# Own step tables for the first two and the last three graph pairs, and an fp32 weight product at the head, in a two-layer attention kernel

## The reference

```python
h = max(layernorm(x), 0)
q, k, v = h @ Wq0 + bq0, h @ Wk0 + bk0, h @ Wv0 + bv0          # 8 heads of 64
w = softmax(q @ k.T / 8 + (adj == 0) * -1e9)                    # per head
x = x + w @ v
h = max(layernorm(x), 0)
rel = adj.T * ((h @ Wq1.T) @ (h @ Wk1.T).T)
rel = rel / norm(rel, axis=2)
x = x + rel @ (h @ Wv1.T)
```

## Time and profile before

| | |
|---|---|
| median of three runs | 2456.46 us |
| the profiled execution's own time | 2453.71 us |
| its span | 2451.9 us |
| busy: TensorE, VectorE, ScalarE, GpSimd | 98%, 59%, 69%, 53% |
| granted TensorE clock, mean | 0.994 |
| first matmul, last matmul's group starts | 19.24 us, 2445.97 us |
| share of line 656 (all split products) in the chain that ended last | 78% of the span into B, 7% into O |

### The profile page before, as it was taken

How to read it: one execution, slowest core, us unless ns; L and a number is a source line. 1 busy time by engine, 2 the same in 40 slices (tenths; PEclk the granted TensorE clock), 3 DMA queues, 4 the chain that set the end, 5 groups by cost and what they waited for, 6 DMA issues and landing times.

```text
span 2451.9 us, 53549 instructions
## 1 busy us (share of the span) xinstructions
PE 2395.6 (98%) x19252; PEld 1302.3 (53%) x19252; DVE 1442.2 (59%) x4435; ACT 1686.0 (69%) x4111; POOL 1300.1 (53%) x1159
## 2 busy tenths in 40 slices
PE   6999999999999999999999999999999999999986
PEld 3455555555555555555555555555555555555543
DVE  5555666655666556666555665555665556665543
ACT  5677676677676677776677776677766777776762
POOL 3555555555555555555555555555555555555541
PEclk9999999999999999999999999999999999999998
DMA  7566666666777566776566775666766666766552
GB/s 207 115 121 136 138 151 138 124 127 136 145 147 135 120 130 134 154 141 134 125 134 130 152 144 132 130 130 134 150 135 132 134 133 132 151 138 129 114 112 64
DMA packets 938841, 329.14 MB, mean 134 GB/s; under 512 B 885968, under 2 KB 886224, under 8 KB 938576
## 3 DMA queue, kind: packets, MB, share of 16 engines
q1 hardware_dynamic: 935744, 322.31, 63.2%
q10 hardware_dynamic: 2832, 3.41, 0.4%
HBM read 73.93 MB, written 33.55 MB: 44 GB/s over the span
## 4 chain that ended last, share of the span: by engine, by line
PE 93%; DVE 2%; ACT 2%; DMA 1%; issue 1%; POOL 1%; ACTq 0%; DVEq 0%; SPq 0%
PE B L656 78%; PE S L729 7%; PE O L656 7%; DMA probs_t<-halves 1%; ACT probs L451 1%; PE B L686 1%; DVE stats L515 0%; ACT h L391 0%; ACT halves L459 0%; POOL v L341 0%; DVE masked L590 0%; POOL halves L345 0%; ACT h_halves L398 0%; ACTq L377 0%; POOL sq_pow L366 0%
## 5 line engine op out<-in xcount | busy, mean ns | idle before, releaser
L345 POOL TENSOR_TENSOR halves<-probs,halves 128x512 f16<-128x512 f32 x512 | 597.7, 1167 | 572.9 <-ACT halves L459 572.5
L451 ACT ACTIVATE probs<-masked,neg_max 128x256 f32<-128x256 f32 x1024 | 508.5, 498 | 213.1 <-DVE neg_max L590 211.3
L590 DVE CUSTOM_DVE_ANT_0 masked<-S,mask 128x256 f32<-128x256 f32 x1024 | 386.7, 417 | 127.2 <-PE S L729 126.6
L331 POOL TENSOR_TENSOR h_halves<-h,h_halves 128x512 f16<-128x512 f32 x256 | 295.1, 1158 | 160.5 <-ACT h_halves L398 160.5
L656 PE MATMUL B<-wv,h0t 128*128 128x512 f16 x1536 | 354.9, 381 | 19.2 <-DMA h0t<-h_halves 19.2
L656 PE MATMUL B<-wvt,h1t 128*128 128x512 f16 x1536 | 349.6, 381 | 9.6 <-DMA h1t<-h_halves 9.5
L656 PE MATMUL B<-h0t,wq 128*128 128x512 f16 x1536 | 353.2, 380 | 0.4 <-DVE wk L545 0.4
L656 PE MATMUL B<-h0t,wk 128*128 128x512 f16 x1536 | 352.5, 379 | 0.0
L656 PE MATMUL B<-h1t,wm 128*128 128x512 f16 x1536 | 346.9, 379 | 0.0
L459 ACT ACTIVATE halves<-probs 128x512 f16<-128x512 f32 x512 | 322.5, 630 | 16.1
L656 PEld LDWEIGHTS O<-v,probs_t 128*128 128x128 f16 x6144 | 248.9, 98 | 131.9 <-DMA probs_t<-halves 9.3
(11 more groups left out here) (70 smaller groups left out, 2932.6 us busy)
## 6 DMA issues: line engine op xcount, KB each, us to landing
x_in<-in_x_dram SPq DMA_DIRECT2D x128, 256.0 KB, 3.1
x_res<-in_x_dram SPq DMA_DIRECT2D x128, 256.0 KB, 3.3
out_dram<-result SPq DMA_DIRECT2D x128, 256.0 KB, 3.4
probs_t<-halves SPq DMA_TRANSPOSE x512, 2.9
h0t<-h_halves SPq DMA_TRANSPOSE x128, 3.2
h1t<-h_halves SPq DMA_TRANSPOSE x128, 3.3
rv<-in_L_gnn_Wv_dram ACTq DMA_DIRECT2D x2, 512.0 KB, 5.6
rq<-in_L_gnn_Wq_dram ACTq DMA_DIRECT2D x2, 512.0 KB, 7.4
```

Source lines behind the costliest of these rows:

```text
L331: nc.gpsimd.tensor_tensor(h_halves[:, n, 1, :], h[:, n % 2, :], h_halves[:, n, 0, :], ALU.subtract).then_inc(h_low[layer], 1)
L345: nc.gpsimd.tensor_tensor(halves[:, n % RING, 1, :], probs[:, n % 2, :, :].rearrange("p t n -> p (t n)"), halves[:, n % RING, 0, :], ALU.s ...
L451: ins = nc.scalar.activation(probs[:, n % 2, i, :], masked[:, n % 2, i, :], ACT.Exp, bias=neg_max[:, n % 2, i:i + 1], scale=-1.0, accum_ou ...
L590: ins = nc.vector.tensor_tensor_reduce(out=masked[:, n % 2, i, :], in0=S[n % 4][:, i, :], in1=mask[:, i, :], scale=SCORE, scalar=BIG, op0= ...
```

## The change

Pairs 0, 1, 29, 30 and 31 get tables of their own; all others keep theirs. The product Wq1^T Wk1 moves to TensorE's very beginning, with its operands loaded first, feature slice by feature slice, and accumulated in the four `S` banks; its two halves are made in pair 0 as steps `setup_rq` at slots 2 to 5. The other weights are staged in other free buffers, and Wv1 in `h1t`. The three bias loads go from ScalarE's queue to SP's. ScalarE does the layer norm of all four tiles before the weights. In the last pair the transposed h of layer 1 goes to the half of `h0t` that pair 30 used, and the residual is added onto `x_in`, which that pair still holds, so its four `x_res` loads go. Counters of steps (`P_COUNT`, `R_COUNT`, `H_COUNT`) are taken from the order instead of from the place in the table. Lines that only use these, or `h1_buffer` and `res_buffer` in place of the old names, are left out here, and of the tables a line each stands.

```diff
+    OPENING = {("rq", 0): 2, ("rq", 1): 3, ("rq", 2): 4, ("rq", 3): 5}
...
+    PRODUCT_0 = {("v", 0): 0.5, ("v", 1): 1, ("q", 0): 1.5, ("k", 0): 2.5, ("v", 2): 5, ("v", 3): 7,
...
+    MULTIPLIED_0 = [10, 12.5, 14, 14.5, 17.5, 17.5, 22, 22.5, 24.5, 25, 26.5, 27.5, 30.5, 31, 32, 33]
...
+    PRODUCT_31 = {("q", 0): 0.5, ("k", 0): 1, ("v", 0): 2.5, ("q", 1): 4, ("v", 1): 4.5, ("k", 1): 6,
...
+    MULTIPLIED_31 = [7.5, 7.5, 9, 9.5, 10.5, 11.5, 11.5, 14, 15, 15.5, 16, 17, 19, 19, 19, 20.5]
...
+    def timetable(p):
+
+        product_at, scored_at, masked_at, multiplied_at = PRODUCT_AT, SCORED, MASKED, MULTIPLIED
+        layer0, layer1 = LAYER0, LAYER1
+        if p == 0:
+            product_at, scored_at, masked_at, multiplied_at = ({**PRODUCT_AT, **PRODUCT_0}, SCORED_0, MASKED_0,
+                                                               MULTIPLIED_0)
+            layer0 = {**LAYER0, **LAYER0_0}
+        elif p == 1:
+            product_at, layer0 = {**PRODUCT_AT, **PRODUCT_1}, {**LAYER0, **LAYER0_1}
+        elif p == PAIRS - 3:
+            product_at = {**PRODUCT_AT, **OUT_29}
+        elif p == PAIRS - 2:
+            product_at, layer1 = {**PRODUCT_AT, **PRODUCT_30}, {**LAYER1, **LAYER1_30}
+        elif p == PAIRS - 1:
+            product_at, scored_at, masked_at, multiplied_at = PRODUCT_31, SCORED_31, MASKED_31, MULTIPLIED_31
+            layer0, layer1 = {**LAYER0, **RESIDUAL_31}, LAYER1_31
+        tensor = [(slot, 0, "scores", m) for m, slot in enumerate(scored_at)]
+        tensor += [(slot, 1, kind, n) for (kind, n), slot in product_at.items()]
+        tensor += [(slot, 2, "pv", n) for n, slot in enumerate(multiplied_at)]
...
+        others += [(slot, 5, "setup_rq", n) for (kind, n), slot in OPENING.items()]
...
+    def in_order(engine):
 
         order = []
         for p in range(-1, PAIRS):
-            for i, (slot, place, kind, n) in enumerate(steps):
-                if p >= 0 and not (p == 0 and slot < 0):
-                    order.append((PERIOD * p + slot, place, p, i, kind, n))
-                elif p < 0 and (kind, n) in SETUP:
+            for i, (slot, place, kind, n) in enumerate(timetable(p)[engine]):
+                if p >= 0:
+                    if not (p == 0 and slot < 0) and not (p > 0 and kind == "setup_rq"):
+                        order.append((PERIOD * p + slot, place, p, i, kind, n))
+                elif (kind, n) in SETUP and kind != "rq":
...
+    SETUP = list(OPENING) + [st for st in RELATE if st[0] == "rv" or st == ("rel", 0)]
...
-        stage = [as_weight(rv), as_weight(rq), x_res[:, 1, :, :]]
+            return buffer.rearrange("p a k t -> p (a k t)").bitcast(fp32).rearrange("p (k t) -> p k t", k=KT)
+
+
+        stage = [as_weight(rv[:, :, :, :]), as_weight(v[:, 1, :, :, :]), x_res[:, 0, :, :]]
+        stage_q, stage_k = as_weight(rq[:, :, :, :]), x_res[:, 1, :, :]
+        stage_v = as_weight(h1t[:, :, :, :])
+
+        def setup_bank(kind, n, p):
+
+            return S[n].rearrange("p t n -> p (t n)") if kind == "setup_rq" else B[BANK[kind, n, p]]
+
+        def h1_buffer(p):
+
+            return h0t[:, PAIRS % 2] if p == PAIRS - 1 else h1t
+
+        def res_buffer(p):
+
+            return x_in if p == PAIRS - 1 else x_res[:, p % 2, :, :]
...
-                dst = h0t[:, pair % 2] if layer == 0 else h1t
+                dst = h0t[:, pair % 2] if layer == 0 else h1_buffer(pair)
...
+            sp.dma_start(bq[:, :], bq0.rearrange("(m p) -> p m", p=P),
+                         allow_slow_non_contiguous=True).then_inc(small_loaded, 16)
+            sp.dma_start(bk[:, :], bk0.rearrange("(m p) -> p m", p=P),
+                         allow_slow_non_contiguous=True).then_inc(small_loaded, 16)
+            sp.dma_start(bv[:, :], bv0.partition_broadcast(P)).then_inc(small_loaded, 16)
             sp.dma_start(adj_in, adj.rearrange("(t p) n -> p t n", p=P)).then_inc(adj_loaded, 16)
             for n in range(TILES):
                 turn_h(0, n, 0)
-            for n, w in enumerate((wv1, wq1, wk1)):
-
-                sp.wait_ge(w_low, 2 * n + 2)
-                sp.dma_start(stage[n], w.rearrange("(t p) n -> p t n", p=P)).then_inc(w_loaded[n], 16)
+            sp.dma_start(stage_v, wv1.rearrange("(t p) n -> p t n", p=P)).then_inc(wvt_loaded, 16)
...
+                elif kind == "x_res" and p < PAIRS - 1:
+
+                    if p == 0 and n == 0:
+                        sp.wait_ge(w_low, 6)
                     if p == 1 and n == 0:
-
-                        sp.wait_ge(setup_done, NSETUP)
-
-                    need(sp, r_done, NRC * (p - 2) + RELATE.index(("out", n)) + 1)
+                        sp.wait_ge(setup_product, KT)
...
-                    if p > 0:
-                        sp.wait_ge(r_product, NRC * (p - 1) + REL_LAST)
+                    if p == PAIRS - 1:
+                        sp.wait_ge(p_product, NPC * p)
+                    elif p > 0:
+                        sp.wait_ge(r_product, max(R_COUNT["rel", 1, p - 1], R_COUNT["rv", TILES - 1, p - 1]))
+                    elif n == 0:
+                        sp.wait_ge(setup_product, SETUP.index(("rv", TILES - 1)) + 1)
                     turn_h(1, n, p)
...
-            act.wait_ge(x_loaded[1], 16)
+            for k in range(KT):
+                if k == 1:
+                    act.wait_ge(x_loaded[1], 16)
+                for buffer, w in ((stage_q, wq1), (stage_k, wk1)):
+                    rows = w.rearrange("(t p) n -> p t n", p=P)
+                    act.dma_start(buffer[:, k, :], rows[:, k, :]).then_inc(wm_loaded[k], 16)
+
...
-            act.dma_start(bq[:, :], bq0.rearrange("(m p) -> p m", p=P),
-                          allow_slow_non_contiguous=True).then_inc(small_loaded, 16)
...
-            for n in range(2):
-                ln_apply(0, x_in, n, 0, h_low[0], 0)
-            for n in range(2):
-                h_high_half(0, n, 0, h_turned[0][n], 0)
+            for first in (0, 2):
+                for n in (first, first + 1):
+                    ln_apply(0, x_in, n, 0, h_low[0], 0)
+                for n in (first, first + 1):
+                    h_high_half(0, n, 0, h_turned[0][n], 0)
             weight_high(0, wv, WS)
-            for n in range(2, 4):
-                ln_apply(0, x_in, n, 0, h_low[0], 0)
-            for n in range(2, 4):
-                h_high_half(0, n, 0, h_turned[0][n], 0)
             weight_high(1, wq, QS)
             weight_high(2, wk, WS)
             act.wait_ge(scaled, 1)
...
+                    if p == 0 and n == 0:
+
+                        pe.wait_ge(setup_done, len(OPENING))
...
+            for k in range(KT):
+                pe.wait_ge(wm_loaded[k], 32)
+                for n in range(KT):
+                    ins = nc.tensor.matmul(setup_bank("setup_rq", n, 0), stage_q[:, k, col(n)], stage_k[:, k, :],
+                                           start=(k == 0), stop=(k == KT - 1))
+                    if k == KT - 1:
+                        ins.then_inc(setup_product, 1)
...
+                        if n == 0 and p >= PAIRS - 2:
+                            for t in range(TILES):
+                                pe.wait_ge(h_turned[1][t], 16 * (p + 1))
```

137 lines of the change are left out of this document (67 added, 70 removed), and 3 rows, old and new, of the table PRODUCT_31.

## The result

| | before | after |
|---|---|---|
| median of the runs | 2456.53 us (2455.41 to 2456.64, 4 runs) | 2421.31 us (2420.59 to 2422.38, 4 runs) |
| ratio, 95% interval | | 0.9861 [0.9849, 0.9873] |
| profiled execution: own time, span | 2453.71, 2451.9 us | 2422.38, 2420.6 us |

A forecast was written before the change was run, and what follows sets the result against it. TensorE bounds the kernel; only the ends can gain. Head 11.7 plus tail 26.0 is 37.7 off the 2451.9 us span: 2414.2, 2416.0 by own time, plus 2.75 for the median 2418.8, say 2419; range 2411 to 2426.

The forecast's parts named there:

- stalls from there to k2.1: Head, from pair 0's first scores to product k of tile 2, pair 1: TensorE waits of 9.2 us, bounds 5 to 16.
- k2.1, gain: Head: product k of tile 2, pair 1, comes at 106.8 instead of 118.52 us, a gain of 11.7.
- small waits: Tail: 2.5 us set aside for small waits and a stretch at half clock.
- tail gain: Pair 31 early, with pair 30's layer 1 behind it, saves 26.0 us; bounds 20.5 to 31.
- the 2.62 for wvt: Head: TensorE's 2.62 us wait for the wvt half goes, as pair 1's layer norm no longer precedes it on VectorE.
- 14.1 us as moved work: Head: the fp32 product's 16 matmuls, 14.1 us, move to the front, where TensorE waits anyway.
- chain 17.1, so 1.6 us stay bare: Tail, last pv to first h1 tile: chain of 17.1 us, 15.5 covered by pair 30's rv and out, 1.6 uncovered.
- A: Rival at the head: all 16 fp32 matmuls run at half clock, 28.2 us, scores start 8.4 late; 2427 us, chance 0.12.
- B: Rival in pair 0: without the product's cover up to 9 us more are lost, head gain 3; 2428 us, chance 0.12.
- C: Rival in pair 31: units squeezed too far, waits of 10 us in all; 2429 us, chance 0.10.
- D: Rival in pairs 0 and 31: transpositions run singly, 6.0 us a unit, 71 us more; 2490 us, chance 0.03.
- B's second half: Head loads: DMA engines alternate between queues, so x tile 1 lands at 5.2 us; otherwise 4.2, the head 1 us earlier.

The follow-up runs named there:

- e8: Changed kernel with the fp32 product back in pair 0, its loads and prologue as before, own tables for pairs 0 and 1 kept; ratio 0.9880 to the kernel before.
- e9: Changed kernel with pair 31's last residual addition on VectorE instead of GpSimd; 2419.33 us, ratio 0.9856 to the kernel before.
- e12: The kernel of e9 run a second time; 2417.68 us, ratio 0.9853 to the kernel before.
- e5: The changed kernel run again, unedited, with a new profile; ratio 0.9860 to the kernel before.
- e11: Changed kernel with the edits of e9 and e10 together; ratio 0.9862 to the kernel before.
- e3: Changed kernel with the common table for pairs 0 and 1, the fp32 product still at the head; ratio 0.9898 to the kernel before.
- e4: Changed kernel with pair 31's h1 back in its old buffer h1t; ratio 0.9859 to the kernel before.
- e10: Changed kernel with ScalarE's eviction of rv3.30 put ahead of tile 1's h in pair 31; ratio 0.9855 to the kernel before.

## Why the prediction came out

| step | predicted | measured |
|---|---|---|
| fp32 product, start and end | 5, 22 | 6.04, 22.3 |
| v0.0 | 24.2 | 23.73 |
| scores0.0 | 38.0 | 37.12 |
| stalls from there to k2.1 | 9.2 | 8.0 |
| k2.1, gain | 106.8, 11.7 | 104.76, 13.8 |
| from k2.1 to scores3.1 | 0 | -1.2 |
| from there to scores3.30 | 0 | -3.2 in this execution |
| scores3.30 to the end of pv15.31 | 69.2, and 2.5 for small waits | 72.85 |
| from there to rq0.31 | 21.2 | 23.6 |
| rq0.31 to the end | 33.2 | 33.7 |
| tail gain | 26.0 | 22.0 |
| time | 2419 | 2421.31 |

**Head.** The sum held within 2.1 us and step by step. The product took 16.30 us against 16.7; its first matmuls were slow by 2.2 us in all, and the rest at 0.88. x tile 1 was in by 5.6, the loads were issued by 11.97 (12.5 forecast). ScalarE reached the first h at 13.29 and wv at 19.53, 6.2 behind it as forecast:

```profile
13.29 1.52 ACT L473 ACTIVATE h<-x_in,shift,rstd 128x512 f32<-128x512 f32 x2
...
19.53 1.99 ACT L487 ACTIVATE wv<-rv 128x1024 f16<-128x1024 f32 x2
```

Of the stalls, scores1.0 (1.42 for 1.5), v0.1 and scores1.1 (1.06 idle and no half speed, for 3.5) were placed right, and the 2.62 for wvt went. At k2.1 the gain is 13.8, at scores3.1 11.2 to 12.5; in the first execution 1.2 us were lost on the way, 1.06 of them as idle time ahead of rv0.0 at 111.52, which the sum did not have. What was wrong is the credit: the prediction booked 14.1 us as moved work and treated the tables as what keeps the loss small. e8 shows that the tables give 6.1 (by ratio 8.8) with the product left where it was. The sum could not show this, since it counted TensorE's whole work from scores0.0 on, and is the same by either route.

**Tail.** The mechanism held, and the tail paid 4.0 us less than forecast. Three terms. First, 3.7 us of small waits in pair 31 where 2.5 were set aside for the whole tail; the longest, 1.26 for h1t at 2344.24, was not foreseen. Second, 2.4 us more to rq0.31, and this is the step that was wrong: "chain 17.1, so 1.6 us stay bare". The first transposition landed about 18.1 behind pv15.31, because rel_halves took 1.85 and not 0.88 beside GpSimd (e9, e12). And the outs that should have covered the chain waited for their own operand, rv3.30, whose eviction the order on ScalarE puts behind tile 2's h; together 3.75 us idle and 1.33 at a lower speed, so that rv0.31 started 20.9 and not 17.1 behind pv15.31. Both count for the end. In e5 the last transposition is issued by 2382.91, and by the 2.0 to 2.1 us of e9 to e11 rq0.31 could have started at 2385.0; it started at 2386.09, behind the slow outs. So an estimate from these rows gives 1.1 us to the outs and their clock, and the rest of the 2.4 to the chain. Third, 0.5 behind rq0.31.

**Middle.** Nothing moved there, as said. The 3.2 us of the profiled execution are scatter (e5), and another term hid them: I added 2.75 us for the median over the profiled execution, but the changed kernel's profiled execution is 1.07 above its median. With 6.4 us less gain in the traces (2.1 more at k2.1, then 1.2, 3.2 and 4.0 less) and 3.8 from this, 2418.8 becomes 2421.4. The agreement of the time is thus in part luck; by the ratios the change is worth 34.1 us and the forecast was 37.7.

**Rivals.** A is refuted: all 16 matmuls took 16.30 us, not 28.2. Its first five records (two make a matmul) took 3.96 us instead of 2.2 (5 x 0.44), with a granted clock of 1.00:

```profile
6.04:10.00 3.96, 3.96 (x5) 1.80 (x6) 2.26 (x9) 0.00 (x0) 1.03 (x1) 1.00 0.97 274
```

That 1.00 does not settle it, since the kernel before has 1.00 too from 19.20 to 24.30, where v0.0's 12 matmuls took the 5.03 us that the prediction read as the lower clock. In five other traces (e3, e4, e10, e11, e12) TensorE waited another 0.24 to 1.19 us for a load behind the first eight records, so the loads do hold it up; how much of the 2.2 us is the clock stays open.

B holds for a product moved without own tables (e3: a head gain of 2.9, for the 3 that B gave, and 8.4 to 9.7 us less than in e5 and the changed kernel), not for the kernel as it is. C: pair 31's waits sum to 3.7, not 10. D is refuted by the length of pair 31. For B's second half, the queues: x tile 1 landed at about 5.6, and the forecast's 5.2 was nearer than 4.2, but no run here separates the cause.
